# A second buffer for the first one-hot block and four PSUM banks for side jobs in the count build of a graph network kernel

## What is computed

```python
z = h @ W.T + b
e = leaky_relu(concat([z[src], z[dst]]) @ aW.T + ab)[:, 0]
ex = exp(e - segment_max(e, dst)[dst])
alpha = ex / segment_sum(ex, dst)[dst]
h = segment_sum(alpha[:, None] * z[src], dst)
```

## Time and profile before

| what | before |
|---|---|
| median of 3 runs | 4453.6 us (4448.56 to 4459.53) |
| span of the profiled execution, first to last instruction | 4502.7 us |
| granted TensorE clock, mean of the span | 0.859 |
| PE busy, share of the span | 3132.8 us, 70% |
| DVE busy | 3224.2 us, 72% |
| ACT busy | 1435.4 us, 32% |
| POOL busy | 1405.7 us, 31% |

### The profile page before, as it was taken

How to read it: one execution, slowest core, us unless ns; L and a number is a source line. 1 busy time by engine, 2 the same in 40 slices (tenths; PEclk the granted TensorE clock), 3 DMA queues, 4 the chain that set the end, 5 groups by cost and what they waited for, 6 DMA issues and landing times. The chain is left out here.

```text
span 4502.7 us, 84639 instructions
## 1 busy us (share of the span) xinstructions
PE 3132.8 (70%) x29061; PEld 2437.5 (54%) x29061; DVE 3224.2 (72%) x7791; ACT 1435.4 (32%) x2737; POOL 1405.7 (31%) x1198
## 2 busy tenths in 40 slices
PE   0087777777238348158499985588888769959995
PEld 0054444444102112112499984287888769959995
DVE  7766666665489699699577763377767579967886
ACT  0034444444025125035399981233333200000000
POOL 0055555555264454554000000266666300000000
PEclk9978888888569679579699996599999879979997
DMA  8845555545458358267377740111111024413331
GB/s 323 322 129 143 153 144 148 157 131 149 147 172 264 114 166 263 88 200 246 106 221 221 222 148 12 56 24 23 24 23 24 14 67 111 109 28 102 88 91 47
DMA packets 413507, 587.19 MB, mean 130 GB/s; under 512 B 76420, under 2 KB 301787, under 8 KB 412709
## 3 DMA queue, kind: packets, MB, share of 16 engines
q1 hardware_dynamic: 366005, 447.98, 34.2%
q0 software_dynamic: 37728, 66.91, 5.5%
q10 hardware_dynamic: 9360, 66.90, 3.7%
HBM read 340.05 MB, written 234.93 MB: 128 GB/s over the span
## 5 line engine op out<-in xcount | busy, mean ns | idle before, releaser
L846 POOL DMA_INDIRECT slots<-bc_rec,idx x496 | 484.6, 977 | 410.4 <-ACT bc_rec L807 294.4
L1284 POOL DMA_INDIRECT rp_rows<-rel_rows,slot_rel x390 | 412.1, 1057 | 431.7 <-POOLq L118 182.3
L1106 PE MATMUL psum<-a_probs,z 128*65 128x512 f32 (+1 forms) x1050 | 445.7, 557 | 145.0 <-DVE a_probs L1039 145.0
L1320 DVE TENSOR_SCALAR rp_hot_src<-rp_key_rows,lane 128x384 bf16<-128x384 f16 x1560 | 383.5, 317 | 202.0 <-issue 88.5
L1534 PE MATMUL psum<-rel_pieces,rp_hot_src 128*128 128x192 bf16 x4680 | 452.1, 249 | 94.3 <-issue 75.8
L1074 ACT ACTIVATE a_tops<-a_tops,a_s_low 128x1024 f32<-128x1024 f32 (+2 forms) x300 | 284.1, 947 | 569.6 <-DVE a_tops L1030 569.1
L1534 PEld LDWEIGHTS psum<-rel_pieces,rp_hot_src 128*128 128x128 bf16 x4680 | 390.4, 99 | 128.8 <-issue 107.0
L483 POOL DMA_INDIRECT slots<-h,idx x192 | 327.6, 1706 | 352.3 <-DMA h<-recs 304.1
L1106 PEld LDWEIGHTS psum<-a_probs,z 128*65 128x65 f32 x1050 | 121.8, 137 | 469.4 <-DVE a_probs L1039 301.5
L703 DVE TENSOR_SCALAR bc_first_t<-bc_ramp,bc_key_t 128x128 f16<-128x128 f16 x500 | 136.5, 273 | 307.8 <-PE psum L729 172.7
L1030 DVE SCALAR_TENSOR_TENSOR a_tops<-table,a_s_rest,big 128x1024 f32<-128x1024 f32 (+2 forms) x300 | 309.3, 1031 | 32.8 <-DMA big<-shift_rows 32.8
(11 more groups left out here) (438 smaller groups left out, 6855.1 us busy)
## 6 DMA issues: line engine op xcount, KB each, us to landing
a_counts<-edge_counts SPq DMA_DIRECT2D x150, 512.0 KB
slots<-big ACTq DMA_DIRECT2D x65, 1005.0 KB
ep_rec<-slots SPq DMA_DIRECT2D x65, 1005.0 KB, 6.2
edge_counts<-bc_counts SPq DMA_DIRECT2D x12, 3125.0 KB
hot_rows<-ep_hot_src SPq DMA_DIRECT2D x325, 96.0 KB, 4.5
sp_hot_src<-hot_rows SPq DMA_DIRECT2D x325, 96.0 KB, 2.0
sq_hot_src<-hot_rows SPq DMA_DIRECT2D x325, 96.0 KB, 2.0
a_counts<-edge_counts SPq DMA_DIRECT2D x75, 282.5 KB
```

What stands on the lines that cost most here:

```text
L846: pool.indirect_dma_start(k.slots, bass.IndirectOffsetOnAxis(k.idx[:, first + t:first + t + 1], 0), rec[:, j, t, :], None).then_inc(scatte ...
L1106: last = nc.tensor.matmul(sums[:, a:b], k.z[:, s, 0:D + 1], probs[:, a:b], start=s == 0, stop=True, skip_group_check=True)
L1284: pool.indirect_dma_start(rows[:, n % ROW_SLOTS, s, 0:width], None, table, bass.IndirectOffsetOnAxis(k.slot_rel[:, at:at + 1], 0))\
L1320: last = v.tensor_scalar(hot_src[:, n % HOT_SLOTS, rel, :], key_rows[:, n % 2, :], k.lane[:, rel:rel + 1], None, ALU.is_equal)
```

## The change

The memory of the old `first` buffer goes; two buffers for the first block now lie in `k.acc`, seen as fp16. A block needs 4 x (625 + 128) = 3012 values for each partition, two need 12048 bytes of the 13100 that `acc` has. DVE fills buffer at % 2 in window at, and waits for the products of two windows before. The clearing of `acc` moves from `setup` to the end of `build_counts`, after the last use of the buffers. The window sums get two sets of banks (0 to 3) where there were three, and the side jobs four banks (4 to 7) where there were two, so that a side job waits for the job four before it, and the products of a window for ACT's copy of the window two before it where it was three.

```diff
@@ setup
-                v.memset(k.acc[:, :, :], 0.0)
@@ build_counts
-    PS_SETS = 3
+    PS_SETS, SIDE_BANKS = 2, 4
...
-        first_s, first_t = sb("first_s", [P, BUILD, COLS], FP16), sb("first_t", [P, BUILD, P], FP16)
+        early = k.acc[:, :, :].rearrange("p t c -> p (t c)").bitcast(FP16)
+        FIRST = BUILD * (COLS + P)
+        first_s = [early[:, y * FIRST:y * FIRST + BUILD * COLS].rearrange("p (u c) -> p u c", c=COLS) for y in range(2)]
+        first_t = [early[:, y * FIRST + BUILD * COLS:(y + 1) * FIRST].rearrange("p (u c) -> p u c", c=P) for y in range(2)]
@@ side_job, last_marks
-                return at, 6 + at % 2
+                return at, 2 * PS_SETS + at % SIDE_BANKS
-            return g * SIDES + at + PRE_JOBS - SIDES, 6 + at % 2
+            job = g * SIDES + at + PRE_JOBS - SIDES
+            return job, 2 * PS_SETS + job % SIDE_BANKS
@@ block.vector
-                    if at:
-                        dve.wait_ge(first_used, at)
-                    one_hots(at, first, first_s, first_t, first_ready)
+                    if at >= 2:
+                        dve.wait_ge(first_used, at - 1)
+                    one_hots(at, first, first_s[at % 2], first_t[at % 2], first_ready)
...
+                dve.wait_ge(first_used, NWIN)
+                v.memset(k.acc[:, :, :], 0.0)
@@ block.tensor, edge_products
-                    if job >= 2:
-                        pe.wait_ge(side_taken, job - 1)
+                    if job >= SIDE_BANKS:
+                        pe.wait_ge(side_taken, job - SIDE_BANKS + 1)
@@ block.tensor, windows
-                    products(y, first_s, first_t, True, first_used)
+                    products(y, first_s[at % 2], first_t[at % 2], True, first_used)
```

More of the change, by code:

```diff
@@ L669, in side_job @@
                 at = REC_ORDER.index(x)
-                return at, 6 + at % 2
+                return at, 2 * PS_SETS + at % SIDE_BANKS
             at = SIDE_ORDER.index(x)
-            return g * SIDES + at + PRE_JOBS - SIDES, 6 + at % 2
+            job = g * SIDES + at + PRE_JOBS - SIDES
+            return job, 2 * PS_SETS + job % SIDE_BANKS
         def last_marks(i):
-            return NGROUP * SIDES + i + PRE_JOBS - SIDES, 6 + i % 2
+            job = NGROUP * SIDES + i + PRE_JOBS - SIDES
+            return job, 2 * PS_SETS + job % SIDE_BANKS
         def window_range(eng, at):
```

## The result

| what | before | after |
|---|---|---|
| median of 6 runs each, on one chip | 4455.35 us | 4435.18 us (4431.19 to 4445.12) |
| ratio | | 0.9954 [0.9942, 0.9966] |
| span of the profiled execution | 4502.7 us | 4433.8 us |
| granted TensorE clock, mean | 0.859 | 0.855 |

The change takes 20 us off where 118.5 were forecast. The two spans must not be subtracted: the profile before seems to come from another chip.

What follows compares the result with a forecast made beforehand. It took the count build to be paced by PE's third side job waiting for a bank ACT must empty. Banks -147.5, `more` +30 and tail -1 gave -118.5 us, from 4453.6 to 4335 us; range 4260 to 4415.

Steps and rivals of the forecast that it cites:

- Banks, -147.5 us: Count build: four side banks take away all PE's waits for ACT, 119.0 + 28.5 us.
- Rival D: Count build: PE's recorded idle is only partly idle, a third of 147.5 us real; gain about 45 us, 4409; chance 0.11.
- Given back to `more`, +30 us: Before `more` products: PE waits for DVE's single-buffered one-hots, 30 times at 1.0 us; bounds 0 and 71 us.
- rival B: Count build: without idle PE's clock stays up, some 5.2 us a window; 250 us go, 4204; chance 0.12.
- Nothing gained by double-buffering: Side banks: by the skill page's rule the sum would be 0, the wait going on elsewhere; 4454; chance 0.04.
- Two first buffers, 0: First block's one-hots: a second buffer saves 0, earning only below a period of some 5.6 to 5.9 us.
- Memset, 0: Clearing moved from `setup` to the build's end: 0 both times, covered by DVE's waits; without cover +2.8 us.
- Two sum sets, 0: Window sums: two bank sets for three cost 0, unless ACT falls a window behind.
- Rival E: Marks' store: ACT waits for its landing in faster windows, eating the gain from 14.8 us on; 4470; chance 0.03.
- The rate of 6.2 us a window: Count build, sign of the forecast: first products of all windows over some 772 us, 6.2 us each.

Runs made afterwards that it cites:

- e9_before_third: The kernel before, unchanged, run again for a profile on a chip where PE completes late: 4459.9 us, one run.
- e10_after_again: The change, unchanged, run again on a chip where before takes 4456.8 us: 4438.1 us, ratio 0.9951 to before.
- e3_more_two: The change plus a second buffer for the `more` one-hots, taken by the window's parity: 4453.0 us, ratio 0.9911 to before.
- e2_first_only: Kernel before with only the two first buffers and the moved memset, keeping three sum sets and two side banks: 4493.1 us, ratio 1.0005.
- e6_narrow_before: Kernel before with 64 + 64 columns in all products but those of a window's first tile: 4175.6 us, ratio 0.9989 to before.
- e5_narrow: The change with 64 + 64 columns in all products but those of a window's first tile: 4112.9 us, ratio 0.9835 to before.

## Why the prediction was wrong

- **Banks, -147.5 us: the step that failed.** The waits went as predicted (147.5 to 15.9 us), but the time did not go with them. "I take all the waits of PE for ACT away" took PE's recorded idle as room, to be saved but for what came back before `more`. On one chip 138.9 us of bank waits went and 112.6 came back, 66.9 before `more` products and 45.7 as issue (`e9_before_third`, `e10_after_again`). With `more` relieved as well (`e3_more_two`) the idle became issue, for some 20 us of gain. What stands behind it is PE's late work: ACT and DVE were released up to 8 us after the drawn end, and PE was drawn idle meanwhile. That it is the reason is argued, not shown by taking it away on one chip. It is supported by the chip without lateness, where the change gained 63 and 106 us in kernels with equal cuts. Those gains are larger than the bank waits of the same kernels (23.4 and 42.7 us), so rows of waits don't size the gain there either.
- **Rival D** had the cause nearly right from what the prediction itself read out of the earlier trace rows. It had 0.11, and its 45 us were still twice too many. Its sign, as written, did not come: PE's idle did not fall by 147 us while the time fell by less; it changed its name.
- **Given back to `more`, +30 us.** The place was right, the size not: 61.9 us of PE's waiting in 46 waits, where the sum had 30 of 1.0 us, taken from a row of DVE's waits; it lies within the bounds of 0 and 71. In the window shown the late release makes it (DVE idle for 7.07 us), more than DVE's 2.2 us a block. With a second buffer the wait went, and some 20 us with it.
- **What the sum lacked:** 48.7 us more of issue, and the clock. In the stretch shown the granted clock falls to 0.50 behind the single instructions. From 223 to 1060 us its mean went from 0.83 to 0.80, and from 0.86 to 0.81 in `e9_before_third` and `e10_after_again` (rival B forecast the reverse). The Trainium skill's page "TensorE: Matmul & The Clock Gate", section "Why this matters for your kernels", says that gaps in PE's work bring the half clock back; the trace agrees, with products of 2.24 us after the gap and 1.24 before it.
- **Nothing gained by double-buffering.** The Trainium skill's page "TensorE: Matmul & The Clock Gate", section "HAM oscillation", by which the sum was 0, lay nearer to the 20 us measured on these chips than the sum from the rows did.
- **Two first buffers, 0: right in time** (1.0005 on the old banks; on four banks about 5 us, not clear of noise). The reason was not: it was to earn only below 5.6 to 5.9 us a window, yet with one buffer and four banks PE waited 68.2 us for it at some 7 us a window. **Memset, 0: right** (in `e2_first_only` with the buffers): DVE waits 15.1 us for the next stage behind it. **Two sum sets, 0: right as far as shown**: 1.1 us of waits for ACT's copy. **Rival E** fell: the time went down, and the one wait of ACT for the marks' store between 230 and 1120 us took 2.9 us.
- **The rate of 6.2 us a window** was reached and passed where PE is on time: 5.0 us in the kernels with four banks and light edge jobs. Before was not profiled on such a chip and the change not timed there; the pairs with equal cuts differ by 63 and 106 us, near 118.5 but below it. That the change alone gains this there is an inference.

What stays open is what makes PE late on some chips. Product columns, a fifth of the matmuls, the attribute loads and the length of PE's program are ruled out as its main cause; the fp32 products, the turned marks, POOL's scatters and the chip itself are not.

## What to carry to other kernels

PE's recorded idle time can be counted as room only if the engines that wait for PE are released when its instructions are drawn to end. So compare the start of the first waiter with the drawn end before any wait is put into a sum. If PE waits for ACT, and ACT waits for late work of PE, the time is PE's own; taking the buffer limit away then moves it, here to the next single buffer and into issue. Check a clock column of exactly 1.00 against the durations of equal matmuls. And run before and after on more than one chip: what gains 0.5% on one may gain more on another.

## What was unexpected in the hardware

- One kernel took 4177 to 4493 us on different chips. More than half of it lies in the build: it lasts 901 us (223 to 1123.7 us) in `e9_before_third`, and 734 us (to 956.7 us) in `e6_narrow_before`, which takes as long as before on its chip (0.9989). What follows the build takes 3334 and 3227 us.
- Where PE is late, its completions come up to 8 us after the drawn end (8.9 in `e3_more_two`), and at times it takes one instruction per 0.71 us, weight load or matmul, 64, 113 or 512 columns alike. It happens with the core's DMA engines full (share 1.01 to 1.12 above) and also with them nearly idle, as at 880 us of the change's trace (the DMA share is the last column but one):

```profile
880.00:882.00 2.00, 0.31 (x2) 0.10 (x1) 0.00 (x0) 0.04 (x1) 0.33 (x1) 0.58 0.10 34
```

- The names that a profile gives such waits are the mark of it: waits of ACT for the sums are named after a DMA of another stage in the traces with lateness (125.6 us in the change's), and in none of those without.
- With product columns cut, `e5_narrow` ran nearly its whole build at the lower clock (0.55 from 230 to 930 us), and still took 66 us less than before on its chip.
